# A causal convolution moved into projection weights, and the last state sums turned, in a fused conv, scan and DCT kernel

## The reference, cut to what matters

```python
xz = x @ in_proj_w.T
xi, z = jnp.split(xz, 2, axis=-1)                  # 128 channels each
xc = causal depthwise conv of xi, 4 taps, + conv_b
xs = silu(xc)
dt, Bm, Cm = split(xs @ x_proj_w.T)
delta = softplus(dt @ dt_proj_w.T + dt_proj_b)
# scan over the 1024 pixels, for each of 16 states n
h = exp(delta * A[n]) * h + (delta * xs) * Bm[n];  y += h * Cm[n]
y = (y + xs * D) * silu(z)
out = y @ out_proj_w.T
```

## Time and profile before

| | |
|---|---|
| median of 3 runs | 987.98 us (987.41 to 989.94) |
| profiled execution | 989.86 us |
| its span | 987.7 us |
| mean granted TensorE clock | 0.948 |
| busy: PE, DVE | 807.9, 798.5 us |
| busy: ACT, POOL | 564.3, 519.6 us |
| DVE scans (L1603) | 128, 290.1 us |
| DVE causal convolution (L1559, L1562) | 32 instructions, 8 images |

### The profile page before, as it was taken

The page is one execution under the profiler, slowest core; times in us unless marked ns, Lnnn a source line. Parts: engine busy times, 40 slices in busy tenths (PEclk is TensorE's granted clock), DMA queues, the critical chain, the costliest instruction groups (busy, mean ns, idle before and its releaser), DMA issues. The chain is left out here.

```text
span 987.7 us, 10385 instructions
## 1 busy us (share of the span) xinstructions
PE 807.9 (82%) x3787; PEld 509.9 (52%) x3787; DVE 798.5 (81%) x652; ACT 564.3 (57%) x983; POOL 519.6 (53%) x240
## 2 busy tenths in 40 slices
PE   3999998976576778799999999797756677869995
PEld 2444443443365667656545444344335577865654
DVE  6899885377998998998899888447699999899832
ACT  3755231146479897786667332114456979878712
POOL 2015993110498786876111699311048869677730
PEclk8999999999799999899999999898869989989988
DMA  3000000001535454443000000000123445444400
GB/s 104 1 0 0 0 0 1 0 1 48 133 134 180 153 181 163 140 159 130 20 0 11 12 0 0 1 0 1 48 89 127 175 148 184 160 148 154 146 21 22
DMA packets 32878, 73.95 MB, mean 75 GB/s; under 512 B 15544, under 2 KB 15680, under 8 KB 32832
## 3 DMA queue, kind: packets, MB, share of 16 engines
q1 hardware_dynamic: 31424, 72.04, 21.9%
q0 software_dynamic: 320, 1.05, 0.4%
q10 hardware_dynamic: 1088, 0.26, 0.1%
HBM read 70.71 MB, written 2.62 MB: 74 GB/s over the span
## 5 line engine op out<-in xcount | busy, mean ns | idle before, releaser
L338 POOL TENSOR_TENSOR arena<-arena 128x1024 f32<-128x1024 f32 x128 | 304.8, 2392 | 99.1 <-DVE arena L1603 72.8
L1603 DVE TENSOR_TENSOR_SCAN arena<-arena,ps 128x1024 f32<-128x1024 f32 x128 | 290.1, 2282 | 20.6 <-ACT arena L857 9.6
L857 ACT ACTIVATE arena<-arena 128x128 f32<-128x128 f32 (+3 forms) x424 | 157.1, 446 | 91.3 <-DVE arena L1530 75.3
L857 ACT ACTIVATE arena<-arena,Amat 128x1024 f32<-128x1024 f32 x128 | 145.3, 1145 | 62.0 <-DVE arena L1603 61.1
L544 PE MATMUL ps<-mat,arena 128*128 128x128 f32 x528 | 74.8, 288 | 51.6 <-DVE arena L1603 49.9
L857 ACT ACTIVATE arena<-ps 128x1024 f32<-128x1024 f32 (+2 forms) x62 | 56.1, 917 | 93.7 <-PE ps L414 29.0
L717 PE MATMUL ps<-arena,mat 128*128 128x512 f32 x240 | 106.3, 592 | 0.0
L586 PE MATMUL ps<-mat,arena 128*128 128x128 f32 x768 | 104.7, 281 | 1.1 <-POOL arena L338 0.8
L544 PEld LDWEIGHTS ps<-mat,arena 128*128 128x128 f32 x528 | 60.9, 144 | 67.3 <-DVE arena L1603 53.3
L586 PEld LDWEIGHTS ps<-mat,arena 128*128 128x128 f32 x768 | 90.9, 146 | 3.3 <-POOL arena L338 2.3
L1598 DVE TENSOR_TENSOR ps<-arena,ps 128x1024 f32<-128x1024 f32 x66 | 80.0, 1213 | 3.5 <-PE ps L544 3.5
(11 more groups left out here) (186 smaller groups left out, 1374.3 us busy)
## 6 DMA issues: line engine op xcount, KB each, us to landing
arena<-c_rows SPq DMA_DIRECT2D x128, 512.0 KB, 3.8
out<-arena SPq DMA_DIRECT2D x28, 64.0 KB, 2.2
xres<-x POOLq DMA_DIRECT2D x4, 256.0 KB, 5.3
xres<-x SPq DMA_DIRECT2D x4, 256.0 KB, 4.1
convw<-conv_w SPq DMA_DIRECT2D x1, 576.0 KB
c_rows<-ROWS SPq DMA_DIRECT2D x4, 128.0 KB, 1.9
mat<-mats SPq DMA_DIRECT2D x1, 448.0 KB, 3.7
inw<-in_w SPq DMA_DIRECT2D x1, 256.0 KB
```

The lines of the kernel that those rows point to most:

```text
L338: tt(HC[s % 2], HS[s % 2], CB[s % 4], ALU.mult).then_inc(S("hc"), 1)
L857: return nc.scalar.activation(out_, in_, func, bias=bias, scale=scale, accum_out=accum_out)
L1603: nc.vector.tensor_tensor_scan(HS[q], DA[q], PS[q][:, :], 0.0, ALU.mult, ALU.add).then_inc(S("scan"), 1)
```

## The change

Part 1. At the start the projection's weights for xi are transposed once (`inwT`), and TensorE multiplies them with four diagonal matrices of the taps (`tapdiag`); the four scaled weights go to `tapw`. For the second image of each pair `in_proj` adds four projections of shifted inputs in PSUM, each over both column halves, `causal` handles only the first images, and `silu_x` reads PSUM. Part 2. TURNED holds all four images: every state sum and every z is made turned, and image 3 too is turned back through PS[3]. At the boundary the gate goes between the Sobel sums and differences, and PS[3] is opened behind the last out_proj. Part 3. Before step 26 only odd steps are X_STEPS; the first pair's sums for the mean are taken at step 38; the diffusion block's relu goes to PSUM; normalize(0) stands ahead of add_conv(1).

```diff
+            for t in range(4):
+                ts(blk(tapdiag, t), ident, vecs[:, V_CONVW + 3 - t:V_CONVW + 4 - t], None, ALU.mult).then_inc(S("tapdiag"), 1)
...
-            mm(PS[3][:, 0:P], xdtw[:, :], dtpw[:, :], start=True, stop=True).then_inc(S("dtw_ps"), 1)
+            mm(PS[3][:, 0:P], xdtw[:, :], dtpw[:, :], start=True, stop=True)
+            nc.tensor.transpose(blk(PS[3], 1), inw[:, 2 * P:3 * P], ident).then_inc(S("dtw_ps"), 1)
             pe.wait_ge(S("dtw"), 1)
+            pe.wait_ge(S("tapdiag"), 4)
+            for t in range(4):
+                last = mm(blk(PS[3], 4 + t), inwT, blk(tapdiag, t), start=(t == 0), stop=True, skip_group_check=True)
+            last.then_inc(S("tapw_ps"), 1)
...
-        X_STEPS = [s for s in range(9, SCANS - 1) if (s % 5 in (0, 2, 4) if s < 3 * D_STATE else s % 2 == 1)]
+        X_STEPS = [s for s in range(9, SCANS - 1) if (s % 5 in (0, 2, 4) if 26 <= s < 3 * D_STATE else s % 2 == 1)]
-        TURNED = [0, 1, 2]
+        TURNED = [0, 1, 2, 3]
...
                 for n in range(2):
-                    last = mm(half(PS[2 * k], n), inw[:, 2 * P * b:2 * P * b + P], half(d["XNC"], n), start=True, stop=True)
+                    if b == 0:
+                        last = mm(half(PS[2 * k], n), inw[:, 0:P], half(d["XNC"], n), start=True, stop=True)
+                    else:
+                        for t in range(4):
+                            cut = t if n == 0 else 0
+                            last = mm(PS[2 * k][:, n * BANK + cut:(n + 1) * BANK], blk(tapw, t),
+                                      d["XNC"][:, n * BANK + cut - t:(n + 1) * BANK - t], start=(t == 0), stop=(t == 3))
...
-                transposes(two_images(j, "SZ"), PS[2]).then_inc(S("y_turned"), 1)
+                transposes(two_images(j, "SZ"), PS[3] if j == 3 else PS[2]).then_inc(S("y_turned"), 1)
...
-                if j in TURNED:
-                    y_kept(h, j)
-                else:
-                    pe.wait_ge(S("y_read"), ONE + 4 * h + j + 1)
+                y_kept(h, j)
...
                 out_proj(h, 2)
+                turn_y(h, 3)
                 if h + 1 < HALVES:
                     depthwise(h + 1, 0, 0, 0)
                 out_proj(h, 3)
+                if h + 1 < HALVES:
+                    write_all(PS[3])
...
-                act.wait_ge(S(f"cconv{k}"), 4 * i + 4)
-                av(D[k]["XS"][:, b * L:b * L + L], D[k]["XI"], ACT.Silu, 1.0, vc("m_conv_b")).then_inc(S(f"xs{k}"), 1)
+                if b == 0:
+                    act.wait_ge(S(f"cconv{k}"), 4 * h + 4)
+                else:
+                    act.wait_ge(S(f"xi{k}"), i + 1)
+                av(D[k]["XS"][:, b * L:b * L + L], D[k]["XI"] if b == 0 else PS[2 * k][:, :], ACT.Silu, 1.0, vc("m_conv_b")).then_inc(S(f"xs{k}"), 1)
...
+            act.wait_ge(S("tapw_ps"), 1)
+            av(tapw[:, :], half(PS[3], 1), ACT.Identity).then_inc(S("tapw"), 1)
             for k in range(2):
                 keep_x(0, k, PS[2 * k])
...
-                    av(img(a["X"]), wrapped(a["hw"])[:, :, 1:33], ACT.Relu, par[:, 4:5], par[:, 5:6]).then_inc(S("a_bnout"), 1)
+                    av(img(PS[2 * k + 1]), wrapped(a["hw"])[:, :, 1:33], ACT.Relu, par[:, 4:5], par[:, 5:6]).then_inc(S("a_bnout"), 1)
...
-                    sobel(h, 0)
+                    sobel_sums(h, 0)
                     gate(h - 1, 3)
+                    sobel_differences(h, 0)
...
+                normalize(0, h, 0)
                 add_conv(h, 1)
-                normalize(0, h, 0)
...
+                    if s == 38:
+                        center_sums(0, h, 1)
                     if s == 39:
-                        center(0, h, 1)
+                        center(0, h, 1, sums=False)
```

More of the change, by code:

```diff
@@ L75, in fused_blocks @@
         outw = sb("outw", C)
+        tapw = sb("tapw", 4 * P)
         projw = sb("projw", P)
@@ L514, in in_proj @@
                 wz = inw[:, 2 * P * b + P:2 * P * b + 2 * P]
-                if 2 * k + b in TURNED:
-                    for n in range(BLK):
-                        last = mm(blk(PS[2 * k + 1], n), blk(d["XNC"], n), wz, start=True, stop=True, skip_group_check=True)
-                else:
-                    for n in range(2):
-                        last = mm(half(PS[2 * k + 1], n), wz, half(d["XNC"], n), start=True, stop=True)
+                for n in range(BLK):
+                    last = mm(blk(PS[2 * k + 1], n), blk(d["XNC"], n), wz, start=True, stop=True, skip_group_check=True)
                 last.then_inc(S(f"z{k}"), 1)
@@ L583, in sum_of @@
                 pe.wait_ge(S("hc"), SCANS * h + s + 1)
-                if j in TURNED:
-                    for n in range(BLK):
[L586 to L598, removed]
+                for n in range(BLK):
+                    last = mm(blk(PS[3], n), blk(HC[s % 2], n), ident, start=first and n % 4 == 0, stop=True,
+                              is_transpose=True, skip_group_check=True)
+                last.then_inc(S("sum"), 1)
+                if first:
+                    for n in range(BLK):
+                        mm(blk(PS[3], n), blk(two_images(j, "XS"), n), diagD[:, :], start=False, stop=True, skip_group_check=True)
             def turn_y(h, j):
                 pe.wait_ge(S("y_read"), ONE + 4 * h + j + 1)
-                transposes(two_images(j, "SZ"), PS[2]).then_inc(S("y_turned"), 1)
+                transposes(two_images(j, "SZ"), PS[3] if j == 3 else PS[2]).then_inc(S("y_turned"), 1)
             def y_kept(h, j):
@@ L664, in _ @@
                 group_mean(A[k], 0, 0, k)
+            pe.wait_ge(S("tapw"), 1)
             for k in range(2):
@@ L1247, in _ @@
                             small_group_shift(A[s // 18], h + 1, 0, s // 18)
+                    if s == 40:
+                        small_mean(h, 0)
                     if s == 41:
-                        small_mean(h, 0)
                         square(h, 0, 1)
@@ L1276, in _ @@
                     frames(h + 1, 0)
+                    keep_y(h, 3)
                     squares(h + 1, 0)
@@ L1380, in v3, with center_sums @@
                 return t[:, :].rearrange("p (g c) -> p g c", c=C)
-            def center(k, h, g):
-                d, step, n0 = D[k], S(f"lstep{k}"), 4 * h + 2 * g
+            def center_sums(k, h, g):
+                d, step = D[k], S(f"lstep{k}")
                 ps = PS[2] if g == 1 else PS[2 * k]
@@ L1386, in center @@
                 nc.vector.reduce_sum(d["m"][:, :], v3(ps), axis=AX.X).then_inc(step, 1)
+            def center(k, h, g, sums=True):
+                d, step, n0 = D[k], S(f"lstep{k}"), 4 * h + 2 * g
+                ps = PS[2] if g == 1 else PS[2 * k]
+                if sums:
+                    center_sums(k, h, g)
                 if g == 1:
@@ L1539, in add_stage0 @@
                 dve.wait_ge(S("a_bnout"), 2 * h + k + 1)
-                tt(xres[k][:, :], xres[k][:, :], A[k]["X"][:, 0:L], ALU.add).then_inc(S("mid_step"), 1)
+                tt(xres[k][:, :], xres[k][:, :], PS[2 * k + 1][:, :], ALU.add).then_inc(S("mid_step"), 1)
                 dve.wait_ge(S("mid_step"), 4 * h + k + 1)
@@ L1551, in x2_norm, with causal @@
                 group_norm(D[k], h, 2, k)
-            def causal(h, k, b):
-                d, i = D[k], 2 * h + b
-                dve.wait_ge(S(f"xi{k}"), i + 1)
-                if b == 1:
-                    dve.wait_ge(S(f"xs{k}"), i)
+            def causal(h, k):
+                d = D[k]
+                dve.wait_ge(S(f"xi{k}"), 2 * h + 1)
                 w = [vecs[:, V_CONVW + t:V_CONVW + t + 1] for t in range(4)]
@@ L1698, in _ @@
                 variance(0, h, 0)
+                normalize(0, h, 0)
                 add_conv(h, 1)
-                normalize(0, h, 0)
                 x2_norm(h, 1)
-                causal(h, 0, 0)
+                causal(h, 0)
                 center(1, h, 0)
@@ L1707, in _ @@
                 normalize(1, h, 0)
-                causal(h, 0, 1)
-                causal(h, 1, 0)
+                causal(h, 1)
                 relu_x(h, 0, 1)
                 relu_x(h, 1, 0)
-                causal(h, 1, 1)
                 one_plus(h, 0)
```

10 lines of the change are left out of this document (5 added, 5 removed).

## The result

The changed kernel takes 1008.4 us (median of 4 runs, 1008.2 to 1009.9) where the kernel before takes 988.1 (4 runs, 987.4 to 989.9): a ratio of 1.0195 (95% interval 1.0156 to 1.0234), 20.3 us slower. The prediction was 997.0 and reached to 1005. The direction was right, the size was off by 11.4 us. The profiled execution took 1008.2 us (span 1006.3); that of before took 989.9 (span 987.7).

A forecast was written before the change was run, and what follows sets the result against it. No engine was full throughout; a serial TensorE and ScalarE path led into the scans. 20.5 + 1.5 + 0.5 - 3.9 - 3.5 - 2.7 - 2.0 - 1.4 = +9.0 us, giving 997.0, range 985 to 1005.

The forecast's parts named there:

- 2 x 5.15 us in each half: Way into the scans: 12 more matmul records for each second image's projection, serial on TensorE, +20.5 us in all.
- the exponentials wait for the rows' turn, not for VectorE: Before the first scan: VectorE's saved convolutions gain nothing; the rival with VectorE on the path gave 976.5 us, chance 0.06.
- turning holds the clock in steps 56 to 63: Last scan steps: transpositions keep TensorE's clock up; the rival that they don't gave 1027 us, chance 0.02.
- one of the prediction's signs of being wrong: Steps from 48 on: the forecast is wrong if the granted clock falls there.
- the term of steps 56 to 63: Last scan steps, other pair's finish on TensorE: turned sums gain 3.0 us in each half, bounds 0 and 3.15.
- the boundary step: Between the halves: gate ahead of the Sobel differences and turned sums, net -3.5 us, bounds -5.8 and 0.
- 23.7 us behind the gate: Boundary: TensorE's queue after the gate brings the transposition that stood at 502.35 to 498.9.
- the end: Behind the second half's last scan: gate 5.8 us earlier, turn and copy add 1.9, net -3.9 with steps 56 to 63.
- The scaled steps: Scan steps before 26: two more VectorE products against 16 fewer ScalarE copies, -2.0 us for both halves, bounds -5 and +2.
- ScalarE at 46, VectorE at 52.3, so 53.5: Steps 9 to 25: foreseen busy times of both engines, the stretch shrinking from 54.50 to 53.5 us.
- Small moves: First pair's mean summed one step earlier -2.7 us, relu to PSUM -1.4, normalization ahead of the convolution's add +0.5.
- The clock: Rival: longer second-image projections of both halves run partly at the lower clock, 1004 us, chance 0.10.

The follow-up runs named there:

- With the clock held: Kernel before with 12 idle TensorE matmuls ahead of the first pair's second projection and 8 ahead of the last: 983.25 us; single parts were then added to it.
- the moved turn: Changed kernel with TensorE turning the first rows ahead of the last four-tap projection instead of behind it: 999.0 us.

## Why the prediction was right or wrong

**Part 1: right.** It foresaw 2 x 5.15 us in each half, serial on TensorE. With the clock held it is 10.24 in each half, and 21.5 in the whole with the setup, where 22.0 was foreseen. That the exponentials wait for the rows' turn, not for VectorE, is shown by the moved turn, which gave back 9.4 us. Right also that turning holds the clock in steps 56 to 63: a granted clock of 1.00 in all nine traces with turned sums, 24.9 us each. In steps 48 to 55 one of the prediction's signs of being wrong came true in part: the granted clock fell to 0.93 in the window shown, where it had been 1.00. They grew by 0.1 us in the second half and 0.8 in the first; a turned sum pays nothing there.

**Part 2: the term of steps 56 to 63 was mis-sized.** The prediction took VectorE's whole idle time there, 3.0 of 3.15 us, as TensorE's debt. The waits show 1.4 us of TensorE, 1.1 of GpSimd and 0.4 of ScalarE. 1.2 us in each half came back; the waits that stayed and a new one for ScalarE took the rest. 3.6 us of the miss.

**Part 2: the boundary step failed.** Of its 3.5 us, 3.0 were to come from the steps ahead of it, and 0.5 behind the last scan, where 1.4 us (with the clock held) to 2.2 were lost. The step that failed is "23.7 us behind the gate": it costed TensorE's queue at the full clock and as if nothing else were near. It was 25.7 us. The clock falls in the wait for the gate (12 records 1.7 us longer, the turn 0.9), and the gate itself comes 8.3 us behind the last scan, not 7.6. And the transposition at 502.35 was released by VectorE's normalization: with the earlier gate it came 3.6 us forward, and 1.8 of these reached the second half's add.

**Part 2: the end was right as far as it was worked out, and isn't measured behind that.** Gate 3.66 us behind the last scan (3.5 foreseen), reduction 5.9 behind the gate (5.4). From there to the end nothing was to change, and single traces can't tell whether anything did: this stretch takes 32.6 to 36.2 us in eleven traces without turned sums and 34.5 to 36.4 in nine with them, with a mean granted clock between 0.76 and 0.90. By the two traces with the clock held the end is 1.1 us longer where 0.9 less was foreseen, 2.0 us, but that is within this spread. So of the 8.6 us by which part 2 is off in the medians (+1.2 where -7.4 was foreseen), 3.6 + 1.9 stand on steps that the traces agree on, and 3.1 us stay open, the end among them.

**The scaled steps: wrong sign.** The step that failed is "ScalarE at 46, VectorE at 52.3, so 53.5". ScalarE's 51.20 busy us of 54.50 looked like a bound, and 46 was never reached (49.45), but the steps run on the pair of scan and product on VectorE. Of its idle 4.5 us, some 2.8 stand at steps 15 to 17, where the second image begins; 2.3 of them are there in the changed kernel too. The other waits, of 0.3 to 0.4 us, were GpSimd's. +3.1 where -2.0 was foreseen: 5.1 us.

**Small moves.** The mean gained 1.5 us a half, 3.0 where 2.7 was foreseen. Mean and relu together gave 2.9 to 4.5 (4.1 foreseen). The normalization cost 0.5 us by the medians, as foreseen, which is within what they can tell.

**The clock: a rival of the wrong shape.** The prediction asked whether the clock would cost the changed kernel more. The kernel before already paid at least 4.9 us for it (988.1 against 983.25), and idle matmuls give the changed one back 2.5 (1008.4 against 1005.9), in which one half stays at the lower clock. So in the medians it took 2.4 us off the difference. The two profiled executions, 4.5 us above the full clock's 58.3 in one half and 5.5 above 68.55 in both, don't show this; the 2.4 rests on the medians alone.

Together: 8.6 + 5.1 + 1.2 - 0.5 (part 1) - 2.4 (clock) = 12.0, against the 11.3 us between 20.3 and 9.0. That the sum comes out within 0.7 us shows that the parts add up, not that each is explained: 3.1 us of part 2 and 1.0 to 1.5 of the steps have no cause here.

## What to carry to other kernels

Before an engine is relieved, ask of its idle neighbour by whom each wait is ended: ScalarE, busy 94% of a window, did not bound it, and an idle time is owed to several engines, of which the next takes over. Work moved to the engine that stands in the chain costs its full length even when the engine that gives it up is nearly as busy; look for what can be turned round in the queue first (one moved line gave back half). And where single edits of 3 us come out with odd signs, look for a stretch that takes two lengths with the same instructions, hold its clock, and measure again.

## What the runs showed of the hardware

Twelve and eight idle matmuls in gaps of 3.2 and 2.6 us made the kernel 5 to 6 us faster and narrowed its executions from 12 us (29 of them) to 2.2 (12): TensorE's clock otherwise fell to its lower level in one half or in both, in the same gap with the same work ahead of it. A projection of four records takes 1.98 us at the full clock and 3.75 at the lower one. The size of this, half a per cent of the kernel, exceeded each of the small edits that were to be judged (0.5 to 3.1 us), and made a costless one look like a gain of 3.0 us.
